# Graph network with residual layer norm: receiver rows gathered evenly, the first lookup started inside the sort, and five ninths of an edge step in each lookup turn

## The reference

```python
edge_feat = concatenate([h[dst], h[src], rel_pos, distance], axis=-1)
x = silu(edge_feat @ W1 + b1); x = silu(x @ W2 + b2)
scores = (x @ W3 + b3)[:, 0]
mx = segment_max(scores, dst); exp_scores = exp(scores - mx[dst])
alpha = exp_scores / (segment_sum(exp_scores, dst)[dst] + EPS)
msg = h[src] @ Wv * (alpha * node_weight[src])[:, None]
out = layernorm(x + (h + segment_sum(msg, dst)))
```

## Time and profile before

| | |
|---|---|
| median of 3 runs | 926.76 us (926.49 to 930.16) |
| profiled execution | 929.5 us, its span 927.7 us |
| busy share of the span | PE 76%, DVE 69%, POOL 64%, ACT 59% |
| granted PE clock, mean | 0.924 of full speed |
| DMA | 188.46 MB, mean 203 GB/s |

### The profile page before, as it was taken

One profiled execution on the slowest core, in us unless ns is written; L12 is line 12 of the kernel. 1 busy time (PEld: TensorE's weight loads), 2 busy tenths in 40 slices (PEclk: granted clock), 3 DMA queues, 4 the chain that ended last, 5 costly groups with the idle time before them and its releaser, 6 DMA issues.

```text
span 927.7 us, 13366 instructions
## 1 busy us (share of the span) xinstructions
PE 707.7 (76%) x3718; PEld 485.4 (52%) x3718; DVE 640.9 (69%) x2264; ACT 548.5 (59%) x1280; POOL 597.2 (64%) x624
## 2 busy tenths in 40 slices
PE   0001388879998898999898988788999999999610
PEld 0000254546555565666566756566676677666510
DVE  8997788868677676788778978864544454455824
ACT  0000056777667688677677967886665665676440
POOL 3000577777777777777777543467777777775677
PEclk9999998979999999999899988889999999999765
DMA  6000348999999899999999999975443333322131
GB/s 234 0 0 0 67 100 298 316 336 348 325 343 317 295 329 346 327 338 306 289 322 312 321 261 261 293 220 159 111 119 104 95 96 106 106 75 60 65 82 46
DMA packets 120370, 188.46 MB, mean 203 GB/s; under 512 B 21147, under 2 KB 80182, under 8 KB 120296
## 3 DMA queue, kind: packets, MB, share of 16 engines
q1 hardware_dynamic: 86536, 97.47, 35.0%
q0 software_dynamic: 19648, 38.74, 14.8%
q10 hardware_dynamic: 14112, 51.39, 14.5%
HBM read 109.89 MB, written 77.76 MB: 202 GB/s over the span
## 4 chain that ended last, share of the span: by engine, by line
PE 42%; DVE 23%; POOL 11%; DMA 9%; issue 8%; ACT 5%; SPq 1%; ACTq 0%; DVEq 0%; POOLq 0%
PE bank L723 13%; POOL out_rows L446 11%; DMA xin<-in_x 6%; DVE dst L979 4%; PE bank L710 3%; PE bank L665 3%; PE bank L653 3%; PE bank L697 3%; PE bank L690 3%; DMA out_rows<-xin 3%; ACT xin L509 3%; DVE region L786 3%; PE bank L662 3%; PE bank L663 3%; PE bank L644 3%
## 5 line engine op out<-in xcount | busy, mean ns | idle before, releaser
L509 ACT ACTIVATE xin<-xin,drs 128x128 f32<-128x128 f32 x736 | 290.2, 480 | 198.0 <-DVE drs L961 192.0
L442 POOL DMA_INDIRECT hk<-in_x,kg_t x196 | 187.4, 956 | 143.6 <-DVE kg_t L870 84.1
L723 PE MATMUL bank<-hk 128*125 128x512 bf16 x1032 | 247.4, 400 | 7.3 <-DVE snd_i L1036 4.5
L442 POOL DMA_INDIRECT rec<-in_xw,snd_i x196 | 186.2, 950 | 101.6 <-issue 56.7
L446 POOL DMA_INDIRECT out_rows<-hk,sidx_t x196 | 191.0, 975 | 68.9 <-issue 57.3
L723 PEld LDWEIGHTS bank<-hk 128*125 128x125 bf16 x1032 | 147.3, 145 | 99.2 <-issue 21.7
L979 DVE BATCH_NORM_STATS2 dst<-xin 128x6 f32<-128x256 f32 x392 | 135.1, 410 | 7.0 <-DMA xin<-in_x 7.0
L1021 DVE TENSOR_SCALAR hk<-hk,rid 128x512 bf16<-128x512 f16 x344 | 108.9, 378 | 0.1
L558 ACT ACTIVATE hk<-hk,ers 128x128 f32<-128x128 f32 x196 | 79.7, 481 | 0.9 <-DVE ers L961 0.9
L1088 DVE TENSOR_TENSOR hk<-bank,hk 128x512 f32<-128x512 f32 x49 | 33.4, 682 | 65.0 <-PE bank L690 64.9
L710 PE MATMUL bank<-wsel,hk 125*128 125x5 f32 x344 | 46.9, 260 | 35.6 <-DVE hk L1028 35.6
(11 more groups left out here) (203 smaller groups left out, 1004.6 us busy)
## 6 DMA issues: line engine op xcount, KB each, us to landing
xin<-in_x SPq DMA_DIRECT2D x98, 512.0 KB, 7.4
out_rows<-xin ACTq DMA_DIRECT2D x98, 512.0 KB, 6.4
rec_d<-rec SPq DMA_DIRECT2D x49, 258.0 KB, 8.2
region<-rec_d SPq DMA_DIRECT2D x49, 258.0 KB, 4.8
hk<-vc_d SPq DMA_DIRECT2D x43, 256.0 KB, 5.8
krow<-seg_d SPq DMA_DIRECT2D x49, 128.0 KB, 3.9
hk<-in_x,kg_t POOLq DMA_INDIRECT x196, 5.2
rec<-in_xw,snd_i POOLq DMA_INDIRECT x196, 6.0
```

Source lines behind the costliest of these rows:

```text
L442: pool.indirect_dma_start(out=to, out_offset=None, in_=frm, in_offset=bass.IndirectOffsetOnAxis(ap=index, axis=0)).then_inc(done, 16)
L509: ins = nc.scalar.activation(xin[:, j % X_RING, n, :], xin[:, j % X_RING, n, :], ACT.Identity, bias=drs[:, j // 4 % 2, 1, c:c + 1], scale= ...
L723: ins = pe.matmul(bank[7][0:SEL, :], tab[:, k, n, 0:SEL], oh[:, k, :], start=(k == 0 and n == 0), stop=(k == CH - 1 and n == PIECES - 1))
```

## The change

The split of the table moves from POOL to ACT and PE: ACT rounds to bfloat16, PE subtracts the piece from the table in PSUM by a product with the negated identity (`away`), twice. The buffers of the sort's transposes move to other PSUM banks. `one_hot(0)` is issued inside the sort, ahead of the flags; the second `load_places` is issued right behind the first; the last transposes and the copies behind them (`last_flip`, `last_columns`) come in turn 1, behind lookup 0. POOL starts with three `hk`, spreads the others evenly over the 49 `hs` (36 over 49), and gathers each `rt` five groups ahead of its use, with a wait of its own (`take_gathered(k, g)`). `write_rec(g)` comes in turn 3 + 45g/49 (rounded down). The edge chain begins in turn 5, with two parts in two turns of three: five ninths of a step, 63 parts by turn 42, and 82 turns in all.

```diff
-LEAD = 4
-REC_LAG = 7
-E_FROM = 9
+LEAD = 3
+REC_LAG = 3
+E_FROM = 5
+RT_AHEAD = 5
...
         if E_FROM <= turn < LOOKS:
             now.append(left.pop(0))
-            if (turn - E_FROM) % PARTS == PARTS - 1:
+            if (turn - E_FROM) % PARTS > 0:
                 now.append(left.pop(0))
...
+def rec_turn(g):
+
+    return REC_LAG + g * (LOOKS + 2) // G
+
+
 def pool_plan():
-    order = [("hk", g) for g in range(LEAD)] + [("rt", k) for k in range(len(TAKEN))]
+    order = [("hk", g) for g in range(LEAD)]
+    done = LEAD
     for g in range(G):
         order.append(("hs", g))
-        if g + LEAD < HK_LOW:
-            order.append(("hk", g + LEAD))
-    order += [("hk", g) for g in range(HK_LOW, G)]
+        for k, t in enumerate(TAKEN):
+            if max(0, t - RT_AHEAD) == g:
+                order.append(("rt", k))
+        while done < HK_LOW and done - LEAD < (HK_LOW - LEAD) * (g + 1) // G:
+            order.append(("hk", done))
+            done += 1
+    order += [("hk", g) for g in range(done, G)]
...
             load_places(0)
+            load_places(1)
...
             for i, now in enumerate(TURNS):
-                if i + 1 < LOOKS:
+                if 2 <= i + 1 < LOOKS:
                     load_places(i + 1)
...
-                if 0 <= i - REC_LAG < G:
-                    write_rec(i - REC_LAG)
+                for g in range(G):
+                    if rec_turn(g) == i:
+                        write_rec(g)
...
-            cut(nc.gpsimd.tensor_copy(payf[:, :, 0, :], snd_f), 1)
-            cut(nc.gpsimd.tensor_copy(tab[:, :, 0, 0:SEL], whole), 2)
-            cut(nc.gpsimd.tensor_tensor(payr, whole, tab[:, :, 0, 0:SEL], ALU.subtract), 3)
-            cut(nc.gpsimd.tensor_copy(tab[:, :, 1, 0:SEL], payr), 4)
-            cut(nc.gpsimd.tensor_tensor(payr, payr, tab[:, :, 1, 0:SEL], ALU.subtract), 5)
-            cut(nc.gpsimd.tensor_copy(tab[:, :, 2, 0:SEL], payr), 6)
...
+            nc.scalar.activation(away[:], ident[:], ACT.Copy, scale=-1.0).then_inc(S["pieces"], 1)
+            nc.scalar.activation(payf[:, :, 0, :], snd_f, ACT.Copy).then_inc(S["pieces"], 1)
+            act.wait_ge(S["pieces"], 2)
+            nc.scalar.activation(tab[:, :, 0, 0:SEL], flat, ACT.Copy).then_inc(S["pieces"], 1)
+            for n in range(1, PIECES):
+                act.wait_ge(S["left"], n)
+                for h in range(2):
+                    ins = nc.scalar.activation(tab[:, 4 * h:4 * h + 4, n, 0:SEL],
+                                               bank[h][:, 0:4 * SEL].rearrange("p (k n) -> p k n", k=4), ACT.Copy)
+                ins.then_inc(S["pieces"], 1)
...
                 link(vec.tensor_tensor(same, same, row["sidx"], ALU.max))
+                one_hot(0, 0, EARLY)
+                one_hot(0, EARLY, CH)
                 dve.wait_ge(S["t_in"], 16)
...
             for i, now in enumerate(TURNS):
                 if 0 <= i - 1 < LOOKS:
                     take_places(i - 1)
-                one_hot(i, 0, EARLY)
+                if i > 0:
+                    one_hot(i, 0, EARLY)
                 if 0 <= i - 1 < LOOKS:
                     take_words(i - 1)
-                one_hot(i, EARLY, CH)
-                if i == REC_LAG:
-                    take_gathered()
+                if i > 0:
+                    one_hot(i, EARLY, CH)
+                if i == 1:
+                    last_columns()
+                for k, g in enumerate(TAKEN):
+                    if looks(g) + 1 == i:
+                        take_gathered(k, g)
```

More of the change, by code:

```diff
@@ L590, in _ @@
             pe.wait_ge(S["w_in"], 16 * 12)
+            flat = payf.rearrange("p k w c -> p k (w c)")
+            for n in range(PIECES - 1):
+                pe.wait_ge(S["pieces"], n + 3)
+                for h in range(2):
+                    if n == 0:
+                        pe.matmul(bank[h][:, 0:4 * SEL], ident[:], flat[:, 4 * h:4 * h + 4, :], start=True, stop=False,
+                                  skip_group_check=True)
+                    ins = pe.matmul(bank[h][:, 0:4 * SEL], away[:], tab[:, 4 * h:4 * h + 4, n, 0:SEL], start=False, stop=True,
+                                    skip_group_check=True)
+                ins.then_inc(S["left"], 1)
             for n in range(6):
@@ L606, in _ @@
+                    ins = pe.transpose(bank[3][0:1, P:2 * P], row["key"][:, SORTW - 1:SORTW], ident[:])
+                else:
+                    pe.transpose(bank[4][:, 0:1], row["neg"][0:1, 0:P], ident[0:1, 0:1])
+                    ins = pe.transpose(bank[4][:, 1:2], row["neg"][0:1, P:2 * P], ident[0:1, 0:1])
                 ins.then_inc(S["flip_done"], 1)
-            pe.wait_ge(S["flip_ready"], 7)
-            for h in range(2):
-                pe.transpose(bank[7][:, h * SROWS:(h + 1) * SROWS], row["neg"][0:SROWS, h * P:(h + 1) * P], ident[0:SROWS, 0:SROWS])
@@ L618, in _ @@
-            pe.wait_ge(S["tab_split"], 1)
-            pe.wait_ge(S["tab_ready"], 1)
+                    pe.transpose(bank[5][:, h * SROWS:(h + 1) * SROWS], row["neg"][0:SROWS, h * P:(h + 1) * P],
+                                 ident[0:SROWS, 0:SROWS])
+                for k, name in enumerate(("sidx", "seg")):
+                    for h in range(2):
+                        o = k * T + h * SROWS
+                        ins = pe.transpose(bank[6][:, o:o + SROWS], row[name][0:SROWS, h * P:(h + 1) * P],
+                                           ident[0:SROWS, 0:SROWS])
@@ L621, in turn_rows @@
+                ins.then_inc(S["flip_done"], 1)
+                pe.wait_ge(S["wz_in"], 16)
+                pe.wait_ge(S["consts"], 2)
             def turn_rows(g):
@@ L764, in _, with halves, by_row, last_columns @@
             link(vec.memset(cwe[:], 1.0))
+            def halves(v):
+                return v.rearrange("p (h r) -> p r h", h=2)
+            def by_row(v):
+                return v.rearrange("p (r h) -> p r h", h=2)
+            def last_columns():
+                dve.wait_ge(S["flip_done"], 7)
+                vec.tensor_copy(by_row(idx_t[:]), halves(bank[5][:, 0:T]))
+                vec.tensor_copy(by_row(kcol[:]), halves(bank[6][:, T:2 * T]))
+                link(vec.scalar_tensor_tensor(out=by_row(sidx_t[:]), in0=by_row(idrel), scalar=float(N + 1),
+                                              in1=halves(bank[6][:, 0:T]), op0=ALU.add, op1=ALU.min))
+                dve.sem_inc(S["tab_ready"], 1)
             def sort():
@@ L1023, in one_hot @@
                     ins.then_inc(S["oh_ready"], 1)
+            sort()
+            link(vec.tensor_scalar(wvh[:], wvh[:], 0.5, None, ALU.mult))
+            dve.sem_inc(S["consts"], 1)
             def take_places(u):
```

92 lines of the change are left out of this document (34 added, 58 removed).

## The result

The changed kernel takes 931.65 us, median of 20 runs (925.63 to 938.96); the kernel before, beside it on the same chip, 927.05 (918.33 to 936.1). The ratio is 1.0057, 95% interval 1.0033 to 1.0081: slower by half a per cent, where I forecast 912 us. The profiled execution took 935.63 us, with a span of 933.8.

A forecast was written before the change was run, and what follows sets the result against it. POOL's queue of gathers and scatters plus its waits bound the kernel. Next the dense_written flag: lookup 42 at 557.7, ten turns of 103.0, first scatter 661.0, then 252.3: span 913.3, scaled to 912.4 us; range 894 to 925.

The forecast's parts named there:

- POOL's bound: POOL's queue: 416 gathers at 1.25 us, 520 us, so gathers can't end before 613.
- the start: Before lookup 0: the split leaving POOL returns 5.9 us; first gather at 93.1, lookup 0 at 106.8, 10.5 us earlier.
- the flag as the next thing late: SP's dense_written, set behind turn 53: passed at 660.7, first scatter at 661.0, POOL idle some 45 us before.
- I take the middle, rounded down, 10.95 us: Length of turns 5 to 42, between estimates of 10.76 and 11.18 us; puts lookup 42 at 557.7.
- The second estimate: Turn length from PE's work at full clock, 10.52 us, plus 0.66 us on top as before: 11.18 us.
- The first estimate: Turn length from averages before, 11.24 us with two parts and 9.83 with one, in the new mix: 10.76 us.
- the same comes on top now: Turns 5 to 42: waits for DVE's column pick and half clock add 0.66 us a turn again.
- DVE is busy 270 of 355 us: Argument against the slower case: DVE has idle time in the lookup turns; two-part turns averaged 11.24 us, stalls included.
- little or no gain: Rival: turns of 11.2 to 11.45 us, flag at 670 to 680, end 922 to 931 us; chance 0.12.
- slower: Rival: DVE picks late, PE waits and falls to half clock; eight stalls of 5.7 us, end 942 us; chance 0.10.
- I take nothing and keep 15 us for the range: SP's waits for sender groups before row writes: covered by its 220.9 us column-pick wait, so no cost.
- The transfers: Rival: DMA sets the turns; 6.6 MB more by turn 42, 20 us, lookup 42 at 548, 902 us; chance 0.12.

The follow-up runs named there:

- scratch: Changed kernel with all scatters into a scratch tensor, not waiting for the dense-store flag, edge rows missing from the output: 916.37 us, 0.984.
- before_p5: Kernel before with only the number of parts changed, five ninths of a step a turn from turn 9: 945.45 us, 1.017.
- p4_from5: Changed kernel with four ninths of a step a turn, still from turn 5: 931.14 us, 1.006.
- p4_from9: Changed kernel with the edge chain as before the change, four ninths of a step a turn from turn 9: 936.76 us, 1.011.
- odd_half_w2: pairs_odd with half of the dense statistics on DVE and sender rows written two turns later (group 1 one turn): 873.71 us, 0.945.
- rec0_early: Changed kernel with the first read-back of sender rows issued right behind turn 4's place load, ahead of writes and dense loads: 928.35 us, 0.999.
- late_write: rec0_early with sender rows from group 2 on written one turn later: 924.09 us, 0.996.
- odd_63: rec0_early with its 63 parts placed otherwise, two in each odd turn and in six even ones: 911.07 us, 0.982.
- pairs_even: rec0_early with 57 parts in turns 5 to 42, two in each even turn, one in each odd: 901.75 us, 0.968.
- pairs_odd: rec0_early with 57 parts in turns 5 to 42, two in each odd turn, one in each even: 894.84 us, 0.961.

## Why the prediction was wrong

**Right.** POOL's bound and its 1.25 us a gather; the start (first gather 92.8 for 93.1, lookup 0 106.96 for 106.8), all of the 5.9 us back; "ten more turns" (102.7 for 103.0); the flag as the next thing late (scratch); POOL's gap (40.1 for "some 45", both ends late); no waits for rings, and none behind the first scatter and 252.5 for 252.3 us from there.

**Wrong, the deciding step: "I take the middle, rounded down, 10.95 us."** Turns 5 to 42 took 11.40, from lookup 9 on 11.46. The half microsecond has two parts.

The second estimate, PE's work plus what comes on top, gave 11.18, 0.28 too little. Its price of a third of a part more, 0.88 us a turn, was right: before_p5, with 11 parts more in the same 33 turns, has 0.90 us more of PE's work a turn than before. What it left out is the earlier start. PE's full set of work comes only from step 9 on, when the first product with Wv is made: in turn 30 before (409.6 us), in turn 22 now (339.0). Before that a step lacks weights, sums and rows. So with the same 55 parts from lookup 9 on the changed kernel has 10.15 us of PE's work a turn and before_p5 9.89; with 44 parts the earlier start costs 0.2 too (p4_from5 against before). The same fault sat in the base, where it didn't show: the 2.62 us of a part came from turns 38 to 42, and so PE's work before was 8.99 and not 9.64, and on top of it came 1.31 and not 0.66.

The first estimate, by the average turns of 11.24 and 9.83, missed the earlier start too, since 20 of its 33 turns held early steps, and it missed that a two-part turn's price hangs on the turn. Even before's four kinds in the table, in the change's numbers (5, 12, 6, 10), give only 10.85. The middle of two estimates that share an error is no better than either: it took away another 0.23.

What softened this was not in the forecast: 10.95 us was meant for turns 6 to 9 too, and these, with the first and lightest steps, took 9.6 us each. That gave 5.5 us back of the 17 that turns 10 to 42 took too long.

That "the same comes on top now" came out at 1.31 again was luck. The parts alone lowered it to 1.03 (before_p5: PE is idle for 19.7 us and not 26.1), and the rest of the change put 0.28 back, as it did with four ninths (1.51 in p4_from9). It isn't a constant of the machine: the order of the parts, DVE's load and the turn of the writes set it (0.36 in odd_half_w2). My argument "DVE is busy 270 of 355 us" was an average too; its idle time lies in the even turns. Of the rivals the result fits "little or no gain" (922 to 931), with its "11.2 to 11.45 us" turns, and passes it by a hair, at half clock and late picks as in "slower". But these didn't become more: in the whole execution the matmuls of the words (L736) waited 29.3 us for picks, against 35.6 before.

**Wrong: "I take nothing and keep 15 us for the range"**, for queues that are moved past. I counted SP's writes and forgot a move that is in the code and that I had left out of the section on the change too: `load_rec(0)` goes from ahead of the dense loads of its turn to behind them. It cost 5 us in turn 5, and its return put the first scatter 9.3 us earlier (rec0_early). What SP's wait before the writes cost the changed kernel is not settled. Once it can be seen: 3.34 us of a late dense block in turn 15. Writing a turn later won 5.3 us at lookup 42 (late_write). But from lookup 9 on rec0_early had 2.9 us of that wait for 24.2 and was only 1.2 us shorter, and scratch, with 21.0 us for 38.9 in all, had lookup 42 no earlier. The cover I had named, SP's wait for the column pick, seems to have held for most of it: that wait is 224.9 us now for 220.9 before, though the turns are 1.2 us longer, and 240.0 in rec0_early. In the faster variants it no longer held.

**Turns 1 to 4**, taken over at 34.8 us, took 38.4. In the other ten runs with the full look and statistics and the chain in its place they took 35.3 to 38.4, and in this one two of the four looks ran at 7 to 8 us. I should have left this term some 4 us of room; what decides is not settled.

**The transfers** were no bound: 299 GB/s here, and 332 in odd_half_w2, where turns are short.

So of the 20.3 us at the flag 3.6 are turns 1 to 4, 5.9 turn 5 and 11 the others. Not settled: what in the rest of the change, its gathers, its writes or its start, puts the 0.28 us on top; late_write gives 0.17 of it back. And that PE's greater work comes from the complete steps is read from the windows of four kernels, not tried by itself.

A slip without effect: the "some 57 us" that POOL's instructions leave of the span are 60 by their own terms (927.7 - 99 - 520 - 249).

## What to carry to other kernels

A part's price taken from one stretch holds for that stretch: first divide the window's busy time by the turns, take the half clock out, and see whether the parts add up to it. When work is spread over the turns of a loop in which another engine has a period of its own (here a chain every second turn), put it where the engine that gets it is waiting anyway: in two orders of the same 63 parts the kernel was 1.7% apart. Work that starts earlier also reaches its dearest steps earlier. To price a change made of several, build each part of it alone: before_p5 and p4_from9 showed two effects that cancelled in the sum. And read every moved line of an issue queue's program for what it now stands behind, with the engine that waits for it.

## What the hardware showed that I had not expected

TensorE's idle time and what it loses to the half clock go together, but not in a fixed ratio. Between rec0_early and odd_63, with the same work but for a part, 5.7 us of idle time (24.6 against 18.9) came with some 8 us lost to a granted clock of 0.95 for 0.97. But pairs_even and pairs_odd were idle alike (15.6 and 16.0 us) and lost 14 and 7 us (0.96 and 0.98). The DMA engines moved 332 GB/s at a share of 1.00, where the kernel before, at 323 and 0.98, had looked close to its limit. And the same first turns took 35.3 to 38.4 us from one run to another.
